# Attention values product: all four key heads in one place of the step, in four column tiles

## The reference

```python
x = x + 0.5 * ffn(layernorm(x), gate_w, w1, w2)
x = x + attn(layernorm(x), Wq, Wk, Wv, Wo, head_scales, head_dirs)
x = x + 0.5 * ffn(layernorm(x), gate_w, w1, w2)

# ffn: top-1 routing over 16 experts, capacity 320 rows each,
#      gelu(rows @ w1[e]) @ w2[e], times the routing weight
# attn: 8 query heads over 4 key heads of 16 channels, rotary positions, a rank-one
#       term in the scores, a window of 128 keys and the first 4 keys (sinks):
allowed = (j <= i) & ((j < 4) | (j >= i - 127))
attn = softmax(where(allowed, scores, -inf))
out = einsum("bhts,bhsd->bhtd", attn, v)      # the values product
```

## Time and profile before

| what | us |
|---|---|
| median of 3 executions | 582.78 |
| the profiled execution, its own time | 583.51 |
| span of the profiled execution | 581.7 |
| TensorE busy with matmuls | 472.5 |
| VectorE busy | 347.8 |
| ScalarE busy | 321.7 |
| GpSimd busy | 222.4 |

### The profile page before, as it was taken

How to read it: one execution, slowest core, us unless ns; L and a number is a source line. 1 busy time by engine, 2 the same in 40 slices (tenths; PEclk the granted TensorE clock), 3 DMA queues, 4 the chain that set the end, 5 groups by cost and what they waited for, 6 DMA issues and landing times.

```text
span 581.7 us, 10982 instructions
## 1 busy us (share of the span) xinstructions
PE 472.5 (81%) x3044; PEld 310.6 (53%) x3044; DVE 347.8 (60%) x1848; ACT 321.7 (55%) x651; POOL 222.4 (38%) x270
## 2 busy tenths in 40 slices
PE   4445499999274889889898998989899966999991
PEld 3334277777133545556555555655555533777770
DVE  5756223433139778878979789788866563243420
ACT  5345054444134387696877867778786642444440
POOL 3767304545635050320605307152120451054555
PEclk9999999999777599999999999999999996999997
DMA  8831245554236000000000000000000112455540
GB/s 285 270 119 49 72 116 169 169 173 147 88 95 238 0 2 1 20 1 2 19 6 24 16 6 28 6 25 15 29 7 10 41 43 58 133 159 174 158 129 31
DMA packets 44698, 45.55 MB, mean 78 GB/s; under 512 B 4919, under 2 KB 34128, under 8 KB 44616
## 3 DMA queue, kind: packets, MB, share of 16 engines
q1 hardware_dynamic: 40040, 36.74, 20.9%
q0 software_dynamic: 4608, 8.22, 4.0%
HBM read 29.22 MB, written 19.17 MB: 83 GB/s over the span
## 4 chain that ended last, share of the span: by engine, by line
PE 47%; DVE 25%; issue 9%; ACT 8%; DMA 5%; POOL 4%; SPq 1%; POOLq 0%; ACTq 0%; DVEq 0%
PE sc L606 12%; PE b L616 12%; DVE junk L1272 10%; PE b L775 3%; POOL slots L1454 3%; PE sc L714 2%; PE sc L542 2%; DMA slots<-pay,slot_i 2%; ACT qT L1055 2%; PE b L686 2%; PE b L595 2%; PE b L630 2%; ACT xn L899 1%; PE sc L740 1%; PE sc L743 1%
## 5 line engine op out<-in xcount | busy, mean ns | idle before, releaser
L1272 DVE CUSTOM_DVE_ANT_0 junk<-sc,cht 128x256 bf16<-128x256 f32 (+1 forms) x256 | 82.2, 386 | 9.8 <-PE sc L714 9.3
L1454 POOL DMA_INDIRECT slots<-pay,slot_i x64 | 63.6, 994 | 37.3 <-issue 20.6
L950 ACT ACTIVATE hT<-sc 128x320 f32<-128x320 f32 x128 | 56.0, 437 | 37.5 <-PE sc L606 26.5
L1499 POOL COPY vaug<-vall 128x64 f32<-128x64 f32 x32 | 8.4, 265 | 176.7 <-PE b L782 112.6
L606 PE MATMUL sc<-enT,w1s 128*128 128x320 f32 x256 | 74.0, 433 | 0.1
L616 PE MATMUL b<-hT,w2s 128*128 128x320 f32 x256 | 73.9, 433 | 0.0
L775 PE MATMUL b<-probs,vaug 128*32 128x256 f32 x448 | 59.8, 386 | 0.0
L1474 POOL DMA_INDIRECT out<-yrow,ytok x40 | 38.9, 972 | 54.5 <-DVE yrow L1245 44.8
L1474 POOL DMA_INDIRECT x<-yrow,ytok x40 | 38.9, 973 | 54.4 <-DVE yrow L1245 44.6
L1028 ACT ACTIVATE probs<-sc 128x1024 f32<-128x1024 f32 x48 | 49.1, 1022 | 17.9 <-PE sc L743 17.9
L606 PEld LDWEIGHTS sc<-enT,w1s 128*128 128x128 f32 x256 | 47.6, 190 | 19.3 <-issue 1.3
(11 more groups left out here) (165 smaller groups left out, 943.5 us busy)
## 6 DMA issues: line engine op xcount, KB each, us to landing
w1s<-in_L_ffn_w SPq DMA_DIRECT2D x32, 256.0 KB, 2.9
w2s<-in_L_ffn_w SPq DMA_DIRECT2D x32, 256.0 KB, 2.8
slots<-fresh SPq DMA_DIRECT2D x16, 330.0 KB, 4.5
rows<-slots SPq DMA_DIRECT2D x16, 330.0 KB, 3.4
xall<-in_L_attn_x SPq DMA_DIRECT2D x8, 256.0 KB, 3.9
xall<-x SPq DMA_DIRECT2D x8, 256.0 KB, 2.7
out<-xall SPq DMA_DIRECT2D x8, 256.0 KB, 2.3
slots<-pay,slot_i POOLq DMA_INDIRECT x64, 2.4
```

The costliest lines, as they stand in the source:

```text
L950: nc.scalar.activation(hT[a][:, f, :], hid[f], ACT.Gelu_apprx_tanh).then_inc(e_gelu, 1)
L1272: ins = v.tensor_tensor_reduce(junk[:, H // 2 * h + i, lo:], sc[h][:, i // G, 2 * P * (i % G) + lo:2 * P * (i % G + 1)], tab16["window"][: ...
L1454: gp.indirect_dma_start(out=slots_d[phase], out_offset=bass.IndirectOffsetOnAxis(ap=slot_i[s][:, t:t + 1], axis=0), in_=pay[s][:, t, :], i ...
```

## The change

The values product of a tile is no longer split into heads 0, 1 (behind the first half of the turned scores) and heads 2, 3 (behind the turned output). All four heads stand at the second place. The order of the matmuls is key block outside, the four heads inside. The waits are the same, all at the second place. In `closing()` the two halves had already stood one behind the other; there only the order of the matmuls changes. No instruction is added or removed on any engine but for waits.

```diff
-            def values(n, t, h, bb):
-
-                if h == 0:
-                    pe.wait_ge(v_copied, n + 1)
-
-                    wait(pe, u_copied, n)
-                pe.wait_ge(st_exp, n * 2 + h + 1)
+            def values(n, t, bb):
+
+                pe.wait_ge(v_copied, n + 1)
+
+                wait(pe, u_copied, n)
+                pe.wait_ge(st_exp, n * 2 + 2)
                 first = 0 if t else 1
                 for kb in range(first, 2):
-                    for j in (2 * h, 2 * h + 1):
+                    for j in range(KV):
                         last = mm(b5[2 * HD * j:2 * HD * (j + 1), 0:G * P], vaug[:, t - 1 + kb, j, :],
                                   probs[t % 2][:, j, kb].rearrange("p g q -> p (g q)"),
                                   start=(kb == first), stop=(t == 0 and kb == 1), skip_group_check=True)
-                if h == 1:
-                    if t:
-                        pe.wait_ge(ps_copied, bb * ST + t)
-                        pe.wait_ge(a_vsink, bb + 1)
-                        last = mm(b5[:, 0:G * P], vsink[:, :], pskT[:].rearrange("r g q -> r (g q)"), start=False, stop=True, skip_group_check=True)
-                    last.then_inc(pv_ready, 1)
+                if t:
+                    pe.wait_ge(ps_copied, bb * ST + t)
+                    pe.wait_ge(a_vsink, bb + 1)
+                    last = mm(b5[:, 0:G * P], vsink[:, :], pskT[:].rearrange("r g q -> r (g q)"), start=False, stop=True, skip_group_check=True)
+                last.then_inc(pv_ready, 1)
...
                         turned_scores(k, t, 0, has(c, TILES))
-                    if has(e, TILES):
-                        values(e, te, 0, be)
                     if has(d, TILES):
                         turn_k(d, td, b, t + 2)
...
                         turn_out(f, b, t - 2)
                     if has(e, TILES):
-                        values(e, te, 1, be)
+                        values(e, te, be)
...
-                for h in range(2):
-                    values(TILES - 1, TB - 1, h, B - 1)
+                values(TILES - 1, TB - 1, B - 1)
```

## The result

| | before | after |
|---|---|---|
| median, same chip, 4 executions each | 583.02 | 601.75 |
| range of the executions | 582.72 to 584.68 | 600.65 to 603.28 |
| span of the profiled execution | 581.7 | 599.7 |
| mean granted clock of TensorE | 0.949 | 0.903 |

The ratio is 1.0308, with a 95% interval of 1.0283 to 1.0332. I had forecast 581.4 us in a range of 579.2 to 583.4: wrong, in sign as well.

A forecast was written before the change was run, and what follows sets the result against it. The chain through attention was taken as the bound, first halves on it six times, second halves twelve. Six gains of 1.74 us less 0.3 gave 1.4 us off the 582.78 us median: 581.4 us, range 579.2 to 583.4.

The forecast's parts named there:

- rival C: One fall of TensorE's clock in attention's repeating part, held 13.7 us, adds up to 4.3 us: 585.7 us; chance 0.06.
- even 2.30 less 1 is more than was there ahead of either fall: Against the clock falling: attention's emptiest 3.4 us stretch found, 2.30 us busy less 1, beats 0.81 and 1.10 before the falls.
- 221 us: ScalarE waits 0.32 us for `turn_k`; without that 0.6 us gained, at most 0.72, until `turn_out` needs the keys' copy.
- 381 us: `turn_out` follows VectorE's output, not the scores; gain 0.15 us.
- 422 us: VectorE waits 0.42 us for the ranks, which need bank b7; gain 0.42 us.
- The repeating part: Between 252 and 382 us no first half is on the chain; the period stays 35.7 us.
- The second place: Four heads for two cost 1.01 us for 0.99; on the chain twelve times, +0.3 us.
- 454 and 461 us: `turn_max` held by bank b6, gain 0.1 us; second exponential behind a normalisation on ScalarE, gain 0.18 us.
- 205 us: The second exponential waits 0.29 us for the turned scores; gain 0.29 us.
- Rival A: At each of the six places another engine was as late, hiding the gain: 582.1 to 583.1 us; chance 0.23.
- B: Five repeating sequences gain 0.5 us each: 578.9 us; milder: clock rise before last experts 3 us earlier gains 1.5; chance 0.15.
- D: In the new order only pairs of heads overlap at the second place, 11 us more: 592 us; chance 0.04.

The follow-up runs named there:

- e1: The kernel after with four filler matmuls (0.86 us of TensorE) at the vacated place of each step: 585.57 us against 582.41, ratio 1.0041.
- e2: The kernel after with one filler matmul of 0.22 us at the vacated place of each step: 592.34 us, ratio 1.0189 to the kernel before.
- e13: The kernel before with the new order in the steps of the last sequence alone: ratio 1.0070 to the kernel before.
- e14: The kernel after with four fillers behind the second turned scores, but the last sequence in the order of before without fillers: ratio 1.0004 to the kernel before.
- e4: The kernel before with both halves at the second place, the turned output between them, so only pairs of heads overlap: 605.66 us, ratio 1.0321.
- e10: The kernel before with half of the first half moved to the second place at t > 0, 0.43 us less TensorE work per step: ratio 1.0054.
- e9: The kernel before, unchanged, profiled again on another chip: ratio 1.0018 to itself.

## Why the prediction was wrong

**What failed** is the weight of rival C, and in it one step: "even 2.30 less 1 is more than was there ahead of either fall". I took the two falls of the kernel before as if they showed how empty a stretch must be. They only show that such stretches are followed by a fall, and nothing about fuller ones. Here are the 3.4 us ahead of each of the five falls in the kernel after, and one stretch that no fall followed:

```profile
261.50:264.90 3.40, 2.38 (x19) 1.69 (x19) 3.19 (x20) 2.68 (x4) 0.00 (x0) 1.00 0.00 0
323.00:326.40 3.40, 1.69 (x24) 0.88 (x24) 3.23 (x19) 2.62 (x7) 2.28 (x3) 1.00 0.07 22
340.00:343.40 3.40, 2.23 (x19) 1.46 (x17) 3.19 (x22) 2.89 (x5) 0.00 (x0) 1.00 0.00 0
381.00:384.40 3.40, 2.31 (x18) 1.63 (x19) 3.19 (x20) 2.73 (x5) 0.00 (x0) 1.00 0.00 0
452.70:456.10 3.40, 2.49 (x22) 1.76 (x19) 2.41 (x15) 2.11 (x4) 0.00 (x0) 1.00 0.00 0
244.50:247.90 3.40, 1.81 (x14) 1.00 (x12) 3.23 (x14) 2.95 (x6) 3.18 (x5) 1.00 0.00 0
```

TensorE was busy 1.69 to 2.49 us ahead of the falls, and a stretch of 1.81 us passed. The kernel before itself passed 2.30 us, and the 2.30 is not its emptiest either, as I had it. This one of the kernel before, in attention, passed too:

```profile
205.70:209.10 3.40, 1.80 (x17) 0.88 (x15) 3.15 (x20) 3.06 (x5) 1.56 (x3) 1.00 0.00 0
```

In the 10 us ahead of any of the five falls TensorE stood idle for at most 1.6 us at a time. Busy time in one such stretch is not what tells them apart, so it could not have excluded a fall. The Trainium skill ("TensorE: Matmul & The Clock Gate", Part 1) says that the clock follows how busy TensorE has been lately; by that rule the change spoke against itself, and the runs agree: e1 and e2 add nothing but work and take back most and some two fifths of the loss.

**The price of C** was a little low for one fall, and wrong for their number. I had up to 4.3 us for 13.7; tiles 20 to 24 lost 40.00 - 34.88 = 5.1 (34.88 us is that sequence in e2, at the full clock). I counted one fall, and there were five with 58.1 us; at 5.1 per 13.7 that is 21.6 us. What the new order gains up to the last scores is 2.4 us, 1.1 of them in tiles 0 to 4, where there also was less time at 0.50. That leaves 19.2 us, close to the 18.8 measured.

**The terms of the sum** held where the clock did:
- 221 us: tiles 4 to 5 in 7.01 us for 7.74, 0.73 us; I had 0.6 and at most 0.72. The wait that takes over is the one named: `turn_out` (now L794) waits for the keys' copy, 7.6 us in 8 waits of the whole run.
- 381 us: tile 23 to 24 in 8.31 for 8.45, 0.14; I had 0.15.
- 422 us: tiles 27 to 29 in 7.74 + 7.93 us for 8.01 + 8.05, 0.39; I had 0.42.
- The repeating part: 35.68 us for 35.68, as said. The 0.13 us that t = 2 gains, t = 3 gives back.
- The second place: 1.00 us for sixteen records; I had 1.01.
- 454 and 461 us lie behind the last scores, where the kernel after has the full clock. The last values product starts 15.97 us behind the last scores for 16.32, so the two places gave 0.35; I had 0.28.
- 205 us can't be told: it lies by a stretch of another clock.

**Rival A** and the milder form of **B** are not decided by the time after. At the full clock, which e2 shows for most sequences, tiles 4 to 8 and 20 to 28 take 1.2 us less than before (0.74, 0.19 and 0.26), so A is out for these. B's 0.5 us in each sequence of the repeating part is out by its period, 35.68 us. For the milder form: the level of 0.50 ends 37.8 us behind the last scores for 40.6, 2.8 us sooner, yet the last experts start only 0.73 us sooner, and 0.35 of that is the two places above. **D** is out by the timeline.

**Open.** Which measure of TensorE's work the clock goes by, and so how much filler is enough. That the last four steps matter for the stretch behind attention was shown on one chip (e13, e14), not explained; the kernel after and e1, with the new order there too, had 13.7 us behind the last scores in their one profile each.

## What to carry to other kernels

Work of TensorE that is hidden behind another engine is not free to remove: it may be what holds the granted clock, and the level reaches everything that TensorE does next. Before taking such work away, look at the stretches that would be left, don't take the falls that a trace has as the border, and price not one fall but one in every repetition. A step that gets longer with the same work has less of it by time (e4). After such a change read the clock's line of the page first; putting meaningless matmuls where the work was is a short test.

## What was unexpected

- By one profile each: with 0.96 us less work in a step of 8.9 us the clock went from no fall in 273 us to five. With 0.74 us less (one filler of 0.22) there were two and one behind the last scores, with 0.43 less (e10) one of 3.4 us.
- At the lower level four column tiles still run at once: 1.94 us for 1.07.
- The kernel before took 583.0 us beside the kernel after, 582.4 beside e1 to e4, and 596.3, 597.2 and 591.8 us in the three sets on other chips. The difference lies outside attention: its second profile (e9) has the first scores at 192.7 us for 182.8, and 93.7 us for 90.0 from the last experts' start to the end, while a sequence takes 35.69 us on either.
